# Attention over 32 heads: one semaphore or two for the adding DMAs, and when a head's loads are issued

## The reference

```python
xn = layernorm(x)
qkv = xn @ qkvw + qkvb                      # 32 heads of 32
scores = einsum('bhqd,bhkd->bhqk', q, k) / sqrt(32)
probs = softmax(scores)                     # 2048 x 2048 for each head
ctx = einsum('bhqk,bhkd->bhqd', probs, v)
attn = ctx @ ow + ob
z = (xn @ A_w.T) * gate                     # gate: softmax of the 16 best of 64 experts
out = x + attn + 2.0 * (z @ B_w.T)
```

## Time and profile before

| what | value |
|---|---|
| median of three executions | 2727.0 us |
| the profiled execution | 2726.84 us |
| its span, first to last instruction | 2724.9 us |
| mean granted TensorE clock | 0.984 |
| PE busy | 2594.6 us, 95% |
| DVE busy | 1636.4 us, 60% |
| POOL busy | 1564.6 us, 57% |
| ACT busy | 1213.9 us, 45% |

### The profile page before, as it was taken

How to read it: one execution, slowest core, us unless ns; L and a number is a source line. 1 busy time by engine, 2 the same in 40 slices (tenths; PEclk the granted TensorE clock), 3 DMA queues, 4 the chain that set the end, 5 groups by cost and what they waited for, 6 DMA issues and landing times. The chain is left out here.

```text
span 2724.9 us, 34698 instructions
## 1 busy us (share of the span) xinstructions
PE 2594.6 (95%) x13032; PEld 1642.2 (60%) x13032; DVE 1636.4 (60%) x2745; ACT 1213.9 (45%) x2268; POOL 1564.6 (57%) x498
## 2 busy tenths in 40 slices
PE   7999999999799999999999999999999999979999
PEld 6888887778555555545545555555554554427887
DVE  8411111111398888888888888878888888714232
ACT  3111111110036666666666666666666666652000
POOL 0111111110148899899888888889988888962111
PEclk9999999999779999999999999999999999999999
DMA  4233334123536767766766766676676677524332
GB/s 147 85 116 115 115 121 126 69 69 96 119 90 142 149 135 146 145 136 138 153 134 134 153 138 140 140 147 136 138 153 133 135 149 141 117 47 165 108 108 96
DMA packets 151797, 342.34 MB, mean 126 GB/s; under 512 B 77232, under 2 KB 102320, under 8 KB 121008
## 3 DMA queue, kind: packets, MB, share of 16 engines
q0 software_dynamic: 22320, 162.54, 30.2%
q1 hardware_dynamic: 129344, 178.05, 23.4%
HBM read 114.31 MB, written 63.44 MB: 65 GB/s over the span
## 5 line engine op out<-in xcount | busy, mean ns | idle before, releaser
L879 DVE TENSOR_REDUCE part_max<-ps_b 128x1 f32<-128x512 f32 x2048 | 1260.2, 678 | 278.8 <-PE ps_b L765 278.8
L867 ACT ACTIVATE probs<-ps_b 128x512 f32<-128x512 f32 x1924 | 984.3, 616 | 557.4 <-PE ps_b L754 555.3
L723 POOL TENSOR_TENSOR psum_p<-psum_p,probs 128x2048 f32<-128x2048 f32 x254 | 1200.7, 4727 | 10.5 <-ACT probs L867 0.3
L765 PE MATMUL ps_b<-kp,qp 96*128 96x512 f32 x2048 | 850.2, 423 | 58.8 <-DVE part_max L879 40.5
L754 PE MATMUL ps_b<-qp,kp 97*128 97x512 f32 x2048 | 839.7, 413 | 5.2 <-ACT probs L867 5.1
L754 PEld LDWEIGHTS ps_b<-qp,kp 97*128 97x128 f32 x2048 | 385.1, 189 | 330.8 <-issue 206.6
L765 PEld LDWEIGHTS ps_b<-kp,qp 96*128 96x128 f32 x2048 | 396.3, 194 | 220.5 <-DVE part_max L879 161.6
L781 PE MATMUL ps_b<-probs,vh 128*32 128x512 f32 x3848 | 466.8, 598 | 0.0
L238 POOL TENSOR_TENSOR wlo<-wraw,whi 128x1024 fp32r<-128x1024 f32 x29 | 69.5, 2397 | 613.6 <-ACT whi L341 613.6
L267 PE MATMUL ps_a<-xhi,whi 128*128 128x512 f32 (+1 forms) x928 | 370.3, 399 | 1.1 <-DVE elo L430 0.9
L267 PE MATMUL ps_a<-xhi,wlo 128*128 128x512 f32 (+1 forms) x928 | 367.6, 396 | 0.0
(11 more groups left out here) (76 smaller groups left out, 1238.9 us busy)
## 6 DMA issues: line engine op xcount, KB each, us to landing
psum_q<-probs POOLq DMA_DIRECT2D x155, 1024.0 KB, 7.4
kp<-qk_scr SPq DMA_DIRECT2D x96, 256.0 KB, 6.8
qp<-qk_scr SPq DMA_DIRECT2D x96, 256.0 KB, 7.4
qk_scr<-ehi SPq DMA_DIRECT2D x16, 1024.0 KB, 3.9
qk_scr<-elo SPq DMA_DIRECT2D x16, 1024.0 KB, 6.7
wraw<-wcat SPq DMA_DIRECT2D x29, 512.5 KB, 7.5
craw<-cz_scr SPq DMA_DIRECT2D x16, 768.0 KB, 5.0
stage<-x SPq DMA_DIRECT2D x16, 512.0 KB, 3.8
```

The lines of the kernel that those rows point to most:

```text
L723: pool.tensor_tensor(acc[:, :], first[:, :], tile(h, t)[:, :], ALU.add).then_inc(pool_done, 1)
L765: pe.matmul(ps[:, ring_bank[u], :], qp[s][0:PACK, tn * P:(tn + 1) * P], kp[s][0:PACK, b * NQ:(b + 1) * NQ], start=True, stop=True).then_in ...
L867: act.activation(tile(h, t)[:, b * NQ:(b + 1) * NQ], ps[:, n % ST_BANKS, :], ACT.Exp, scale=SCALE).then_inc(exp_done, 1)
L879: dve.tensor_reduce(part_max[hn % 2][:, tn, b:b + 1], ps[:, ring_bank[u], :], AX_X, ALU.max) \
```

## The change

The adding DMAs of even heads count on `chained0`, those of odd heads on `chained1`. Each adding DMA waits for the one before it on its own semaphore; the first of a head thus follows the last one of two heads before. `sums` and ACT's wait for a free buffer name the semaphore of their head. On SP the loads of a head are split: keys are issued where all loads were, queries after a further wait for four tiles of the current head's `values`, and values after the stores of the result.

```diff
-        chained = sem("chained")
+        chained = [sem("chained0"), sem("chained1")]
...
-            return 16 * (len(CHAIN_TILES) * h + CHAIN_TILES.index(t) + 1)
+            return 16 * (len(CHAIN_TILES) * (h // 2) + CHAIN_TILES.index(t) + 1)
...
             for h in range(SLOTS):
-                load(h)
+                load_keys(h)
+                load_queries(h)
+                load_values(h)
...
                     sp.wait_ge(pv_done, TT * h)
                     if h + 2 < HEADS:
-                        load(h + 2)
+                        load_keys(h + 2)
+                        sp.wait_ge(pv_done, TT * h + 4)
+                        load_queries(h + 2)
                     store_ctx(h - 1)
+                    if h + 2 < HEADS:
+                        load_values(h + 2)
...
-                wait(pool, chained, chain_count(h, t) - 16)
+                wait(pool, chained[h % 2], chain_count(h, t) - 16)
                 pool.wait_ge(exp_done, 64 * h + 4 * t + 4)
                 pool.sem_inc(cleared, 1)
-                pool.dma_start(psum_q[h % 2][:, :], tile(h, t)[:, :], accum_op=ALU.add).then_inc(chained, 16)
+                pool.dma_start(psum_q[h % 2][:, :], tile(h, t)[:, :], accum_op=ALU.add) \
+                    .then_inc(chained[h % 2], 16)
...
-                pe.wait_ge(chained, chain_count(h, CHAIN_TILES[-1]))
+                pe.wait_ge(chained[h % 2], chain_count(h, CHAIN_TILES[-1]))
...
-                    act.wait_ge(chained, chain_count(hp, tp))
+                    act.wait_ge(chained[hp % 2], chain_count(hp, tp))
```

More of the change, by code:

```diff
@@ L657, in _, with load_keys, load_queries, load_values @@
         def _(sp):
-            def load(h):
-                s = h % SLOTS
-                q_row, k_row = h * HD, h * HD + D
+            def load_keys(h):
+                s, row = h % SLOTS, h * HD + D
                 for r, hl in enumerate((0, 1, 0)):
-                    sp.dma_start(kp[s][r * HD:(r + 1) * HD, :].bitcast(F32), qk_scr[hl, k_row:k_row + HD, :]) \
+                    sp.dma_start(kp[s][r * HD:(r + 1) * HD, :].bitcast(F32), qk_scr[hl, row:row + HD, :]) \
                         .then_inc(kq_loaded[s], 16)
+            def load_queries(h):
+                s, row = h % SLOTS, h * HD
                 for r, hl in enumerate((0, 0, 1)):
-                    sp.dma_start(qp[s][r * HD:(r + 1) * HD, :].bitcast(F32), qk_scr[hl, q_row:q_row + HD, :]) \
+                    sp.dma_start(qp[s][r * HD:(r + 1) * HD, :].bitcast(F32), qk_scr[hl, row:row + HD, :]) \
                         .then_inc(kq_loaded[s], 16)
-                c = h % 4 * HD
+            def load_values(h):
+                s, c = h % SLOTS, h % 4 * HD
                 sp.dma_start(vh[s][:, :, :], v_scr[h // 4].rearrange("p (t c) -> p t c", c=P)[:, :, c:c + HD]) \
```

## The result

The changed kernel took 2760.2 us (median of four runs, 2755.49 to 2764.31) beside 2727.47 us before: a ratio of 1.0113, 95% interval 1.0099 to 1.0127. It is **slower by 1.1%**, 33 us, where I had forecast 29 us faster. The profiled execution took 2764.31 us.

A forecast was written before the change was run, and what follows sets the result against it. PE was 95% busy, but POOL and its adding DMA were taken to pace 23 slow attention beats. The profiled 2726.8 us less 28.7 us, with all other costs 0, gave 2698.1 us; range 2696.5 to 2711 us.

The forecast's parts named there:

- The gain: Attention stage: 23 slow beats, 1205.13 us in all, brought to 51.15 us each, saving 28.7 us.
- The loop of POOL and the landing: POOL's additions plus the wait for tile 14's adding DMA to land: 51.68 us, said to pace the slow beats.
- the floor of 51.15 us: Attention beat, one copy of `raw_ctx` to the next: 51.15 us needed when the adding DMAs are in time.
- the two parts don't add: Two semaphores and fewer loads at the beat's start: the second worth 0 beside the first, alone nearly the same gain.
- the zeros for the queries' wait and for the stores behind it: SP's queue: queries waiting for four tiles of `values`, and `store_ctx` queued behind that wait, each cost 0.
- The values' move: SP's queue: values issued after the stores, ahead of the maxima's load; 0 to 2.8 us a head, taken as 0.
- the price of the load of the negated maxima, "I take 0": PE's first matmul of a head waits for this load; price put between 0 and 2.8 us a head, taken as 0.
- barely issued: Argument against late maxima: long landings come with an adding DMA in full flow, while tile 12's would be just starting.
- the small waits: Rival: maxima 0.3 to 0.5 us late, or a few `sums` waiting; 12 us given back, 2710 us, chance 0.14.
- The slower rival: Values hold up the maxima's load, PE stands 2.8 us in each of 29 heads: 2779 us, chance 0.07.

The follow-up runs named there:

- half the bytes: The changed kernel with tile 12's adding DMA adding only the first 1024 of its 2048 columns: 2704.7 us, ratio 0.9910.
- the run with the hold: The changed kernel with POOL holding tile 12's adding DMA until the load of the negated maxima has landed: 2700.1 us, ratio 0.9892.

## Why the prediction was wrong, point by point

**The gain was right.** The loop of POOL and the landing, the floor of 51.15 us, and 23 beats brought to it: 28.7 us. The changed kernel itself does not show it, but with the collision taken away by one more wait it is measured: 2700.1 beside 2729.4 us, 29.3 us. That the two parts don't add, and that either would do, held as well. So did the zeros for the queries' wait and for the stores behind it. The values' move did no harm (ratio 1.0141 with the values behind the queries, 1.0113 as changed).

**The step that failed is the price of the load of the negated maxima, "I take 0".** I had its deadline right, 4.4 us after the issue, and had even placed tile 12's DMA at +41 to +42.5, right in front of it. But I took 4.3 us as the longest landing and called an adding DMA "barely issued" the harmless case. It is the worst one of those measured, 5.8 us in the usual head, since the whole transfer is still to come. In the kernel before, POOL's lag kept the adding DMA in front of the maxima 4.1 to 8.4 us old in every head, so the earlier trace rows hold no sample of the state that the change creates: they were an observed spread, not a bound. Nor is an adding DMA in full flow what their longest landings have in common, as I had argued against the small waits: with the same 4.9 us between the two, twelve of 21 landed in 2.2 to 2.3 us, and the longest have something else in common (below). What it cost: 1.35 us in the usual beat (52.5 less 51.15), 39 us over 29 beats, and 26 us more, nearly all in the eight worse ones. Of the 26, later landings and a lower clock both have a part (below). Over 29 beats 1548.5 - 1483.4 = 65 us are lost against the floor. Beside the 28.7 gained that is 36 us, and the profiled spans differ by 37.5.

**The slower rival had the right place and the wrong cause.** It named this wait and priced it at up to 2.8 us in 29 heads, 2779 us, with a chance of 0.07. That price takes the maxima to land only with the values, which no run shows. The values, which it blamed, had landed before; that 2760.2 lies within its "up to 2779" is luck. Its price came from the values' longest landing of 14.2 us, taken in a crowd of seven loads and one adding DMA.

**Why the small load is so late.** Issued 1.4 to 1.7 us behind the adding DMA, it lands within 0.6 us of it. For the usual head and one of the worse ones of the changed kernel, first the maxima, then tile 12's DMA:

```profile
L678 SPq DMA_DIRECT2D qp<-neg_max x1: 512/512/512, 1243.0 to 1243.0; - x1
...
DMA to landing us min/median/max: 5.9/5.9/5.9
...
L741 POOL DMA_DIRECT2D psum_q<-probs x1: 872/872/872, 1241.5 to 1241.5; - x1
...
DMA to landing us min/median/max: 7.2/7.2/7.2
```

```profile
L678 SPq DMA_DIRECT2D qp<-neg_max x1: 522/522/522, 1295.7 to 1295.7; - x1
...
DMA to landing us min/median/max: 7.3/7.3/7.3
...
L741 POOL DMA_DIRECT2D psum_q<-probs x1: 865/865/865, 1294.2 to 1294.2; - x1
...
DMA to landing us min/median/max: 8.7/8.7/8.7
```

Counted from the adding DMA's issue, the maxima land at 7.4 and 8.9 us, the DMA itself at 7.2 and 8.7. With half the bytes typical pairs are 4.8 and 4.6. The two are on different queues (the 8 KB packets of the one on `q0`, the 512-byte packets of the other on `q1`), so order on a queue can't be the reason. The page of the profile gives the adding DMAs' queue, and one more that comes up below:

```profile
q0 software_dynamic: 22320, 162.54, 30.1%
...
q8 instruction: 80, 1.31, 0.2%
```

22320 over 155 DMAs is 144. The trace has a record of each packet, with queue, start and size: the 144 are 128 packets of 8 KB and 16 of 4 bytes; a load of the maxima is 16 packets of 512 bytes and 16 of 4. A record names no engine, but the 8 KB packets run sixteen at a time (sixteen start from 1242.89 to 1243.05, the next sixteen from 1243.53 on), so I count eight for each of 16 DMA engines. In the run with the hold, with no adding DMA near, the maxima's packets begin to start 1.2 us after the issue. In the usual beat of the changed kernel they start 4.9 to 5.1 us after it, when all 128 have started or all but one: for the load issued at 1243.03, those of 8 KB start between 1242.89 and 1247.46 and those of 512 bytes between 1247.91 and 1248.10. So the load's own data waits, and not only the report of its landing. The table of the split loads alone shows how much it waits for: the packets that stand ahead by the time it comes, one for each engine at 0.2 us, three at 0.5, five at 0.6, all eight at 1.6. At some 0.64 us a packet, eight take 5.1 us. The rest of the adding DMA goes behind the maxima.

An adding DMA is not one piece that goes ahead as a whole or not at all: at 0.5 and 0.6 us the maxima go between its packets, with 48 and 80 of the 128 started ahead of them. Whether the report of the maxima's landing waits for tile 12's DMA besides, no run shows; the late start of the maxima's own packets, 4.9 us after the issue in place of 1.2, is already 3.7 of the 4.1 us between landings of 5.9 and 1.8. Why all eight packets of an engine stand ahead after 1.6 us, although they take 5.1 us to run, stays open.

**Why some landings are longer still.** Five of tile 12's DMAs in the changed kernel took 8.7 to 9.2 us in place of 7.2, and the maxima behind them over 7 us. In each of the five a 16 KB packet of `q8 instruction` starts 4.8 to 5.6 us after the maxima's issue, as the adding DMA ends. (One more head has one at 5.4 us, when the packets of both DMAs had already gone, and lands in 5.9 us.) The one at 1300.65 takes 0.96 us; the last 8 KB packet starts only at 1301.59, and the last one of the maxima at 1302.34. The same is seen without a collision: in the run with the hold four loads of the maxima took 3.2 to 3.6 us, and exactly these have such a packet 1.1 to 1.3 us after their issue. Four more have one 0.3 to 0.7 us after it and took 2.4 to 2.7 us; the others, with none, took 1.8. In the kernel before, nine loads took 3.6 us or more; eight have a 16 KB packet of `q8` 1.2 to 2.2 us after their issue, and the ninth an 8 KB one of another instruction queue. So the longest landing of the earlier trace rows, the 4.3 us, belongs to a packet of instructions. That these packets are the cause is read from their times alone; no run moved them.

**A part I had not priced: TensorE's clock.** Matmuls right after the pause of 1299.86 to 1303.06, in the changed kernel (columns: stretch, length, then busy us of PE, weight loads, DVE, ACT and POOL, granted clock, DMA share, GB/s):

```profile
1253.12:1305.59 52.47, 48.42 (x257) 26.28 (x258) 42.77 (x73) 33.09 (x65) 44.99 (x14) 0.99 0.68 141
```

```profile
1305.59:1308.73 3.14, 3.14 (x18) 0.74 (x18) 0.80 (x2) 0.28 (x1) 0.93 (x2) 0.62 0.62 125
```

The first figure after the busy times is the clock: 0.99, and then 0.62 on average over 3.1 us, part of it at 1.00 and part at 0.50: the same view has 0.50 for 1304.54 to 1307.94. The 16 matmuls of `values` took 3.06 us there, 1.92 in a usual beat. So this beat's 4.5 us over the floor are 2.9 of waiting (7.3 less 4.4) and 1.6 of slow clock. The granted clock is below 1.00 in exactly the eight worse beats, 0.97 in six and 0.94 in two, and 1.00 over the others. From these means some 17 us of the 26 are an estimate of what the clock took. The kernel before paused PE too, up to 2.1 us at `sums`, and has a granted clock of 1.00 over all its beats. The length of the pause does not settle it: in the changed kernel all five beats whose maxima took over 7 us lost clock, but of the six at 6.0 to 6.4 us three did and three did not, and at 5.8 us none did; with the two semaphores alone one beat at 7.1 us kept 1.00. What makes some pauses cost clock and others not stays open.

## What to carry to other kernels

When a change frees an engine that issues large transfers, list what those transfers will now stand next to: a small load with a deadline just behind a 1 MB transfer cost 1.35 us a head, with what followed from it 2.2, and more than ate the gain. A longest landing in a trace holds only for the spacings of that trace, so look at how long before each sample the last large transfer was issued. Where an engine has time to spare, let it wait for the small urgent load before it issues the big one: one wait on POOL turned 33 us of loss into 29 us of gain.

## What the runs showed that I had not expected

A load of 8 KB issued 1.4 to 1.7 us after an adding DMA of 1 MB on another queue landed together with it, usually 5.8 us after its own issue, against 1.8 us with no adding DMA in flight. Issued 0.2 us after it, it still got through in 3.0 us, behind one 8 KB packet for each engine in place of eight. A single 16 KB packet of an instruction queue went with 1.4 to 1.8 us more on such a load, no adding DMA being near. And a pause of PE could be followed by a stretch of 3.4 us at a granted clock of 0.50: 1.6 us more after the pause of some 3 us looked at above.
